# Selective scan on one Trainium2 core: dt*u of every step brought in by DMA instead of restored by TensorE

## What is computed

```python
def step(h, inp):
    u_t, d_t, B_t, C_t = inp
    dA = jnp.exp(d_t[..., None] * As)
    h = h * dA + (d_t * u_t)[..., None] * B_t[:, :, None, :]
    y = jnp.einsum('bkcn,bkn->bkc', h, C_t)
    return (h, y)
```

## Time and profile before

| | |
|---|---|
| median of three runs | 4128.41 us |
| lowest, highest | 4120.87, 4129.06 us |
| the profiled execution's own time | 4141.09 us |
| its span | 4139.3 us |
| mean granted TensorE clock | 0.88 |
| PE, DVE, ACT, POOL busy | 3704.4, 3223.0, 2433.9, 1570.4 us |
| DMA | 282.21 MB, 68 GB/s over the span |

### The profile page before, as it was taken

One profiled execution on the slowest core, in us unless ns is written; L12 is line 12 of the kernel. 1 busy time (PEld: TensorE's weight loads), 2 busy tenths in 40 slices (PEclk: granted clock), 3 DMA queues, 4 the chain that ended last, 5 costly groups with the idle time before them and its releaser, 6 DMA issues. The chain is left out here.

```text
span 4139.3 us, 114059 instructions
## 1 busy us (share of the span) xinstructions
PE 3704.4 (89%) x49016; PEld 1900.6 (46%) x49016; DVE 3223.0 (78%) x3434; ACT 2433.9 (59%) x4310; POOL 1570.4 (38%) x1171
## 2 busy tenths in 40 slices
PE   6788875899999977699999998959999999999998
PEld 4477742333333333233333334715655655655653
DVE  5565455799898966689988867769889888898881
ACT  2266625444444435344444443618999999999995
POOL 0132210799999930589999870010000000000000
PEclk9799987789888878678888788959999999999999
DMA  5343216222221114322122122531221212222211
GB/s 131 80 75 72 56 33 195 54 68 53 56 64 49 44 46 129 106 58 63 47 59 62 44 57 66 165 79 53 58 58 56 57 52 58 59 56 58 58 42 51
DMA packets 142716, 282.21 MB, mean 68 GB/s; under 512 B 67031, under 2 KB 93783, under 8 KB 135172
## 3 DMA queue, kind: packets, MB, share of 16 engines
q1 hardware_dynamic: 141492, 273.54, 25.1%
q10 hardware_dynamic: 720, 1.38, 0.1%
HBM read 180.62 MB, written 93.67 MB: 66 GB/s over the span
## 5 line engine op out<-in xcount | busy, mean ns | idle before, releaser
L2216 DVE TENSOR_REDUCE l3a_mx<-l3a_mx 128x2 f32<-128x768 f32 x1296 | 1165.1, 951 | 161.5 <-PE l3a_mx L2115 157.4
L2182 ACT ACTIVATE l3a_p<-l3a_s 128x384 f32<-128x384 f32 x2592 | 1180.4, 492 | 114.9 <-PE l3a_s L2129 106.5
L1438 POOL TENSOR_TENSOR l_scan_sc<-l_scan_s,l_scan_repc 128x768 f32<-128x768 f32 x576 | 1031.8, 1809 | 136.8 <-PE l_scan_y L1329 102.2
L1380 ACT ACTIVATE l_scan_da<-l_scan_da,l_k_a 128x768 f32<-128x768 f32 x576 | 503.9, 875 | 777.5 <-PE l_scan_da L1302 777.4
L2129 PE MATMUL l3a_s<-l3a_q,l3a_k 125*32 125x384 f16 x10368 | 805.1, 327 | 5.4 <-DMA l3a_q<-l3a_m 3.6
L1302 PE MATMUL l_scan_dup<-l_scan_dtu,l_k_pick 32*128 32x384 f32 x2304 | 662.0, 650 | 102.9 <-DMA l_scan_dtu<-l_dtp 46.4
L2115 PE MATMUL l3a_mx<-l3a_k,l3a_q 124*32 124x384 f16 x10368 | 673.7, 335 | 58.9 <-DMA l3a_q<-l_qx 31.6
L1302 PE MATMUL l_scan_da<-l_scan_dtu,l_k_pick 32*128 32x384 f32 x2304 | 653.1, 649 | 28.4 <-DVE l_scan_s L1416 23.0
L2141 PE MATMUL l3a_o<-l3a_p,l3a_vh 128*32 128x288 f32 x6912 | 569.9, 405 | 0.4 <-ACT l3a_p L2182 0.4
L2083 POOL TENSOR_TENSOR l3a_norm<-l3a_out,l3a_spread 128x576 f32<-128x576 f32 x24 | 34.5, 1436 | 1343.6 <-DMA l3a_spread<-l_inverses 1343.6
L1396 DVE TENSOR_TENSOR l_scan_bu<-l_scan_dup,l_scan_repb 128x768 f32<-128x768 f32 x384 | 362.7, 944 | 153.7 <-PE l_scan_dup L1302 113.1
(11 more groups left out here) (192 smaller groups left out, 3723.5 us busy)
## 6 DMA issues: line engine op xcount, KB each, us to landing
l3a_q<-l_qx SPq DMA_DIRECT2D x96, 486.0 KB
l_scan_repb<-l_bcp SPq DMA_DIRECT2D x48, 384.0 KB
l_scan_repc<-l_bcp SPq DMA_DIRECT2D x46, 384.0 KB
l_dtp<-l_prep_t SPq DMA_DIRECT2D x16, 864.0 KB, 7.3
l_dup<-l_prep_d SPq DMA_DIRECT2D x16, 864.0 KB, 7.4
l_scan_dtu<-l_dup SPq DMA_DIRECT2D x96, 144.0 KB
l_scan_dtu<-l_dtp SPq DMA_DIRECT2D x92, 144.0 KB
l_y<-l_o_ys SPq DMA_DIRECT2D x24, 288.0 KB
```

What stands on the lines that cost most here:

```text
L1380: act.activation(da_ps[st % 2][:, MID], da_ps[st % 2][:, MID], ACT.Exp, scale=A[:, column:column + 1]).then_inc(exped, 1)
L1438: pool.tensor_tensor(SC[:, st % NSC, :], S[:, n, :], REPC[k % 2][:], ALU.mult).then_inc(weighted, 1)
L2182: act.activation(P[:, k % NP, third * SW:(third + 1) * SW], s_ps[u % NS_PS][:, 0:SW], ACT.Exp)\
L2216: dve.tensor_reduce(MX[:, qt % (NB * KT), 2 * pair:2 * pair + 2], mx_ps[n % NR][:, :, 0:RG], AX_X, ALU.max)\
```

## The change

dt*u no longer goes through PE. For each step SP issues a copy (`spread_du`) that reads the step's 8 rows of dt*u, each 16 times, straight into that step's tile of BU (128 x 768). BU grows from 3 tiles to 9 and takes the place of DUS and BUP as well. The multiply with B is then done in place: on DVE with B as a PSUM operand (b_ps), on POOL with REPB as before. b_ps is filled once per chunk by PE (`restore_b`) from 16 rows of B with a 0/1 matrix state_spread, which DVE makes once. PE's `restore_du`, its order of steps, and ACT's copies of dup go away, and with them the waits between PE, ACT, DVE and POOL over dup. DTU becomes DTB: dt in 64 partitions, B in 16 more.

```diff
-        DTU = [s.sb(f"dtu{i}", [128, NT, HALF]) for i in range(2)]
+        DTB = [s.sb(f"dtb{i}", [64 + NS, NT, HALF]) for i in range(2)]
+        DT = [x[0:64, :, :] for x in DTB]
+        BROW = [x[64:64 + NS, 0:2, :] for x in DTB]
...
-        BU = s.sb("bu", [128, 3, TC])
-        DUS = s.sb("dus", [128, 2, TC])
-        BUP = s.sb("bup", [128, 2, TC])
+        BU = s.sb("bu", [128, NDU, TC])
...
+                def spread_du(st):
+
+                    k, p, d, c, n = place(st)
+                    first = (n % NT) * 32 + n // NT * 8
+                    if st >= NDU:
+                        sp.wait_ge(scanned, st - NDU + 1)
+                    sp.dma_start(BU[:, st % NDU, :], du_dram[p, first:first + 8, span(c)].unsqueeze(1)
+                                 .to_broadcast([8, NS, TC])).then_inc(spread[st % NDU], 16)
...
+                spread_du(0)
                 load_first()
+                for st in range(1, 4):
+                    spread_du(st)
                 load_chunk(1)
+                for st in range(4, NDU):
+                    spread_du(st)
                 for k in range(CHUNKS):
+                    for st in range(k * NN + NDU - 2, (k + 1) * NN + NDU - 2):
+                        if NDU <= st < STEPS:
+                            spread_du(st)
                     if k + 2 < CHUNKS:
                         load_chunk(k + 2)
                     if place(k * NN)[2]:
...
+                def restore_b(k):
+
+                    pe.wait_ge(loaded[k % 2], (k // 2 + 1) * 48)
+                    if k >= 1:
+                        pe.wait_ge(multiplied, k * NG * (NT - 1))
+                    for h in range(2):
+                        at = MID.start + h * HALF
+                        mm = pe.matmul(b_ps[:, at:at + HALF], late.state_spread[64:64 + NS, :],
+                                       BROW[k % 2][:, h, :], start=True, stop=True)
+                    mm.then_inc(b_made, 1)
...
                 def weigh_inputs(st):
                     k, p, d, c, n = place(st)
-                    m = dve_steps_before(st)
-                    dve.wait_ge(rep_loaded[k % 2], (k // 2 + 1) * 32)
-                    if m >= 3:
-                        used = m - 3
-                        dve.wait_ge(scanned, used // (NT - 1) * NT + used % (NT - 1) + 1)
-                    dve.wait_ge(du_made, nth_du[st] + 1)
-                    dve.tensor_tensor(BU[:, m % 3, :], du_ps[:, MID], REPB[k % 2][:], ALU.mult).then_inc(multiplied, 1)
+                    dve.wait_ge(b_made, k + 1)
+                    dve.wait_ge(spread[st % NDU], 16 * (st // NDU + 1))
+                    dve.tensor_tensor(BU[:, st % NDU, :], b_ps[:, MID], BU[:, st % NDU, :], ALU.mult)\
+                       .then_inc(multiplied, 1)
...
-                    pool.wait_ge(du_copied, tr + 1)
-                    if tr >= 2:
-                        pool.wait_ge(scanned, (tr - 2) * NT + GP + 1)
-                    pool.tensor_tensor(BUP[:, tr % 2, :], DUS[:, tr % 2, :], REPB[k % 2][:], ALU.mult)\
+                    pool.wait_ge(spread[st % NDU], 16 * (st // NDU + 1))
+                    pool.tensor_tensor(BU[:, st % NDU, :], BU[:, st % NDU, :], REPB[k % 2][:], ALU.mult)\
                         .then_inc(pool_multiplied, 1)
```

More of the change, by code:

```diff
@@ L1115, in __init__ @@
         self.dsum = s.sb("dsum", [DI, 1])
+        self.state_spread = s.sb("state_spread", [64 + NS, 128])
         self.centre = s.sb("centre", [DI, DI])
@@ L1180, in ssm_scan @@
     LAG = 8
+    NDU = 9
     GP = NT - 1
@@ L1199, in ssm_scan @@
         rep_loaded = [s.sem(f"rep_loaded{i}") for i in range(2)]
-        du_made, dt_made, exped, multiplied, du_copied, pool_multiplied = (
-            s.sem(n) for n in ("du_made", "dt_made", "exped", "multiplied", "du_copied", "pool_multiplied"))
+        spread = [s.sem(f"spread{i}") for i in range(NDU)]
+        b_made, dt_made, exped, multiplied, pool_multiplied = (
+            s.sem(n) for n in ("b_made", "dt_made", "exped", "multiplied", "pool_multiplied"))
         scanned, weighted, piece_summed, y_taken = (
             s.sem(n) for n in ("scanned", "weighted", "piece_summed", "y_taken"))
[L1205 to L1210, removed]
         def place(st):
@@ L1243, in load_first @@
                 def load_first():
-                    for h in range(2):
-                        sp.dma_start(DTU[0][64 + 32 * h:96 + 32 * h, :, :], halves(du_dram, 0, 0, h))\
-                          .then_inc(loaded[0], 16)
+                    sp.dma_start(BROW[0], bc_dram[0, :, span(0)].rearrange("n (h l) -> n h l", h=2)).then_inc(loaded[0], 16)
                     sp.dma_start(REPB[0][:], bc_dram[0, :, span(0)].unsqueeze(0).to_broadcast([8, NS, TC]))\
                       .then_inc(rep_loaded[0], 16)
+                def spread_du(st):
[5 more added lines that the diff above has]
+                                 .to_broadcast([8, NS, TC])).then_inc(spread[st % NDU], 16)
                 def load_chunk(k):
@@ L1253, in load_chunk @@
                     if k >= 2:
[L1254 to L1260, removed]
+                        sp.wait_ge(dt_made, (k - 1) * NN)
+                    for h in range(2):
+                        sp.dma_start(DT[i][32 * h:32 * h + 32, :, :], halves(dt_dram, p, c, h))\
+                          .then_inc(loaded[i], 16)
+                    if k >= 2:
+                        sp.wait_ge(b_made, k - 1)
+                    sp.dma_start(BROW[i], bc_dram[2 * p, :, span(c)].rearrange("n (h l) -> n h l", h=2)).then_inc(loaded[i], 16)
                     if k >= 2:
@@ L1336, in sum_piece @@
                     mm.then_inc(piece_summed, 1)
-                for st in order[0:2]:
-                    restore_du(st)
+                restore_b(0)
                 for st in range(STEPS + LAG):
                     if st < STEPS:
[L1342 to L1346, removed]
+                        restore_dt(st)
+                    if st % NN == NN - 1 and st + 1 < STEPS:
+                        restore_b(st // NN + 1)
                     if st >= LAG:
```

49 lines of the change are left out of this document (17 added, 32 removed).

## The result

| | before | with the change |
|---|---|---|
| median of four runs | 4128.74 us | 4550.23 us |
| lowest, highest | 4120.87, 4154.75 | 4532.31, 4576.62 |
| the profiled execution's own time, span | 4141.09, 4139.3 | 4576.62, 4574.8 |
| mean granted TensorE clock | 0.88 | 0.741 |

The ratio is 1.1014, with a 95% interval of 1.0941 to 1.1087. The forecast was 4606 us, range 4180 to 4870.

A forecast was written before the change was run, and what follows sets the result against it. Step copies on half the DMA engines were taken to bound both scans: 917.3 + 31.7 + 13.5 + 1.9 + 3.6 + 31 = 999 us each, 478 more than 1519.5 for both, giving 4606 us, range 4180 to 4870.

The forecast's parts named there:

- Half the DMA engines carry a copy: Step copies in the scans: outermost source dimension of 8 confines each copy to eight of sixteen engines, share near 0.5.
- 336 copies x 2.73 = 917.3 us bound the scan: DMA queue per scan: 288 spreads and 48 copies of REPB and REPC at 2.73 us each, over POOL's pace.
- copies in SP's waits: Sign that the forecast is wrong: the spreads stand in SP's waits rather than on the DMA engines.
- PE's lost work "would be gain": PE in the scans: loses 662 us of restoring dt*u, 1.1 us each of 576; gain up to 158 us.
- The queue that runs dry, 2.8 us x 11: Copies behind store_y in backward chunks: 12.3 us against a full queue's 9.5, so 2.8 per chunk, 31 per scan.
- my first rival: Sixteen engines: copies at 262 GB/s cost 1.50 us, bare stop of 7.6 us per backward chunk, 4102 us; chance 0.04.
- POOL and DVE unchanged: Multiplies and scans on POOL and DVE keep their number, shape, PSUM operands and durations.
- Eight at their best pace: Step copies on eight engines at 203 GB/s, 1.94 us, each engine reading its own row; 4184 us, chance 0.16.
- Slower still: Step copies at 125 GB/s as the rule once the queue never rests; 4869 us and beyond, chance 0.07.

The follow-up runs named there:

- e3: The changed kernel with e1's edit and dt*u stored twice, so the step copies run on sixteen engines; 4344.82 us, ratio 1.0539.
- e1: The changed kernel with SP's store of y issued one chunk later, behind the next twelve step copies; 4346.79 us, ratio 1.0529.
- e4: The changed kernel with only each scan's first nine step copies issued, tiles multiplied in place again and again; 4261.89 us, ratio 1.0333.
- e2: The changed kernel with dt*u stored twice, outer source dimension 16 in place of 8, the store of y not moved; 4570.1 us, ratio 1.1077.
- e7: The changed kernel with the step copies reading the 16 rows of B or C instead of dt*u; 4615.99 us in one run.
- e6: The kernel of e3 with each restoring of dt issued twice on PE; 4981.6 us, ratio 1.2058.
- e11: The kernel of e3 with REPB and REPC of the next chunk issued behind the eighth copy of a dozen; 4313.38 us, ratio 1.0461.
- e5: The kernel of e3 with each sum over the states issued twice on PE, with weights of a half; 4553.19 us, ratio 1.102.
- e9: The kernel of e5 with REPB and REPC of the next chunk issued behind the eighth copy of a dozen; 4327.08 us, ratio 1.0482.
- e12: e9's order, sums once, smaller PE fillers of zeros added to y, mostly one per step, gate loads moved; median 4162.93 us of 13 runs.
- e10: e9's order, sums once, DVE multiplying with REPB from SBUF, no restoring of B, three PE filler matmuls per step; 4428.29 us, ratio 1.0734.

## Why the prediction was right in time and wrong in parts

The time and the sign came out: 4550 against 4606, 977.4 and 968.9 us per scan against 999. The reason given for it did not.

- *Half the DMA engines carry a copy.* Right: share 0.53 and 0.54 in the stretches of copies; with an outermost 16, e3's 0.81. The Trainium skill, "DMA: Bandwidth & Descriptors", section "Rules for kernel authors", says the same of the outermost dimension, and the trace agrees.
- *336 copies x 2.73 = 917.3 us bound the scan.* This is the step that failed. The copies took 2.21 to 2.37 us in stretches without a stop, 796 us for 336 at most; with that in place of 917.3 the same sum gives 4364, 186 below the measured time. Nor did they bind: once the store was moved DVE waited 35 us for them in the first scan (e1), and twice the engines shortened the scans by 12 us (e3). One of the forecast's own signs of being wrong stood in the profile after, copies in SP's waits: in the first scan SP waited 211.3 us for DVE's scans before it issued them.
- *PE's lost work "would be gain".* Wrong: PE's clock stayed at 0.50, and its remaining work bounds a scan with no copies at all: 135 us over both scans (e4 4262 against 4127). The work was also worth less than the 1.1 us per step of the forecast: 0.3 to 0.6 at half clock, where it overlapped the restoring of dt. The earlier trace rows had the hint: PE busy at 691 of 730 us, and 0.86 and 0.79 for the clock already.
- *The queue that runs dry, 2.8 us x 11.* Right in place, too small: 9.2 us for each of 22 stops, 203 us in all (e1). I had charged only the excess over a full queue's 9.5 us; with copies not the bound, the stop is bare, as in my first rival (7.6), and longer by PE's half clock.
- *POOL and DVE unchanged.* Right: POOL's two operations take 1805 and 1804 ns, DVE's multiply 942.

The account by medians: 4127 before, 4262 with PE at half clock (e4), 4347 with the copies of eight engines (e1), 4550 with the stops. The sum met it by chance: some 240 us of copies too slow over both scans (2 x (917 - 796)) stood in for the clock and most of the stops.

Of the rivals, *sixteen engines* fell with the share of 0.53; given them (e2, e3), the kernel stayed over 240 us above its 4102. *Eight at their best pace* had the copies nearer than the forecast (178 GB/s; 184 in e1), but its reason, that each engine reads a row of its own, fell with e7's one run. *Slower still* had nothing for it.

What stays open is what PE must do for the clock to rise. In the stretches of e4, e6 and e11 PE is busy throughout and stays at 0.50; the clock of the kernel before, e5, e9 and e12 rises and falls, e10's holds. Added work thus brings it up; that the lost work is what the clock misses is argued, not shown: e6 meant to put it back, but its restorings do not overlap as before's did. A second restoring that reads other partitions, as before, would have been the test. The Trainium skill, "TensorE: Matmul & The Clock Gate", section "Part 1: The HAM clock gate (the "warmup" mystery)", has the engine's activity release the throttle; by the profile's busy time alone, e4, e6 and e11 differ from it (500.00 of 500 us at 0.50). Also not tried: e12 with eight engines, which would not store dt*u twice, and fillers in the kernel before.

## What to carry to other kernels

Before work is taken from PE, read the granted clock in the stretch: the clock may go together with the work, and what is left then costs more (here 1.65 us for a restoring in place of 0.92). Look, too, at whether the work to be taken away overlaps work that stays: then little is won. Behind every wait in an in-order DMA queue, list what will be issued after it: a store whose waits of 186 us in a scan cost nothing became some 100 us of stops per scan once urgent copies stood behind it. And a total that comes out right proves none of its terms; the copies were cleared only by moving the store, by giving them twice the engines, and by leaving them out. Where an experiment needs work elsewhere, such as the second store of dt*u, compare the stage and not only the total.

## What the runs showed of the hardware that was not expected

- PE was busy for 500.00 of 500 us at a granted clock of 0.50 (e4, e6, e11), in e11 with no stop of DVE for a copy between.
- Restorings of dt and dt*u, matmuls of 32 rows from different partitions, overlap: eight records take 1.96 us at half clock in the kernel before, 2.93 in e6, where they read the same partitions twice.
- Three matmuls of 128 x 32 by 256 columns took 0.63 us at full clock, three of 128 x 128 by 256 took 1.56 (e10).
- A DVE multiply of two SBUF operands that began 0.19 us after a POOL multiply took 2.44 us, ending 0.82 after POOL's end (e10); with one operand in PSUM it takes 0.93 beside POOL (e5). The Trainium skill, "SBUF — State Buffer", section "Who interferes with whom", says that these two share a port and that the later one waits for the whole of the other; the trace agrees.
- The same eight engines, at a share just over a half, moved 125 to 183 GB/s in the pairs and 166 to 204 in the changed kernels (shares up to 0.56). What sets that pace is open.
